# Order of the matmuls within a product, their waits, and the step that makes w_lo

## The chip, the cores and the metric

The kernel runs on one core of a Trainium2 chip. The metric is the device time in microseconds (us). Before the change it is 218.35 us, the median of three runs (217.48 to 218.54).

## What is computed

The reference is one dense layer of a recommendation model for a batch of 512:

```python
sparse_embed = emb_tables[field_idx[None, :], x_sparse]     # 512 x 26 x 64, gathered rows
z = sparse_embed.reshape(B, N_FIELDS * K)                   # 512 x 1664
gram = jnp.einsum('bik,bjk->bij', sparse_embed, sparse_embed)
inner = gram[:, iu, ju]                                     # 512 x 325, pairs i < j
dnn_in = jnp.concatenate([x_dense, z, inner], axis=-1)      # 512 x 2002
h = jax.nn.relu(dnn_in @ w1 + b1)                           # w1 is 2002 x 2002, float32
out = jax.nn.sigmoid(h @ w2 + b2)                           # 512 x 1
```

## The kernel before

The batch is four tiles of 128 (bt 0 to 3). The contraction is 16 row tiles t: 13 of embedding values (z), 3 of inner products, which also hold the dense features and the bias. The 2002 output columns are two halves h (1002 and 1000), and each half is two PSUM banks q of 500 or 502 columns. A piece is one (t, h) part of w1, 128 x 1002 or 128 x 1000 floats. There are 64 pieces, as all of w1 is read twice: phase A serves bt 0 and 1, phases B1 and B2 serve bt 2 and 3. A product is one piece for one bt; there are 128 of them.

Each product is made in float32r with both operands split into a high and a low part. ScalarE casts a piece into w_hi (L843) and the transposed embeddings into x_hi (L869, for inner products L861); VectorE subtracts to get w_lo (L925, two steps per piece, one for each q) and x_lo (L955). TensorE then runs six matmuls for a product (L1062): for each q, w_hi by x_hi, w_lo by x_hi, w_hi by x_lo. Ahead of them it waits for x_lo of its key (x_split, L1044) and, ahead of each q, for that q's w_lo (w_split, L1060):

```python
pe.wait_ge(x_split, x_lo_count(*key_of(step)))
...
for q, cols in enumerate(CHUNK_COLS[h]):
    pe.wait_ge(w_split, 2 * RANK[n] + q + 1)
    for m, (x, w) in enumerate(((xh, hi), (xh, lo), (xl, hi))):
        last = nc.tensor.matmul(slot[s][:, q * BANK:...], x, w[:, cols], ...)
```

The embedding rows come by 104 gathers (indirect DMAs, L819) on GpSimd's queue, four for a group of four fields and one bt (an arrival), each followed by a small memset (L827) that paces the queue. There are 28 arrivals: the sixteen first hold all of bt 0 and 1 and the last field group of bt 2 and 3. Ahead of the seventeenth, GpSimd waits for the fourth gram round (L817). Ahead of arrival k it also waits until arrival k - 5 has been transposed. VectorE transposes an arrival ("turn", L942), ScalarE makes x_hi of it, VectorE x_lo.

The inner products are eight gram rounds on TensorE (L1035). They read ET, copies of the transposed embeddings made by ScalarE (L874) and VectorE (L960), and write PSUM; ScalarE and VectorE copy the results to G (L887, L973), and they come back as rows of x_in by way of DMAs on SP. Before the first round of a pair of tiles, the finished z part of a cell is moved out of its PSUM slot ("park", L879 and L964). A finished cell is drained by VectorE (relu, times w2, sum: L999).

SP loads the pieces into five raw buffers (w_raw); load m waits until both w_lo steps of piece m - 5 are done (L772). There are seven buffers of w_hi and w_lo; ScalarE's cast of piece m waits until the last product of piece m - 7 is done (L842).

The order of every engine's queue is fixed when the program is built, by a planner (`make_orders`, L214). It plays the engines against each other with given durations (`PE_LEN`, `ACT_LEN`, `DVE_LEN`, L196 to L198), takes among the next six steps of TensorE one whose operands are there (`pe_ready`, L378), and on ScalarE and VectorE the operation that is due first (`wanted`, L412, with a lead for each kind). The program then waits on semaphores for what is really done; a queue never changes its order at run time.

## Time and profile before

| | |
|---|---|
| device time, median of 3 | 218.35 us |
| span of the profiled execution | 227.2 us |
| TensorE matmul busy | 206.2 us (91%), 1340 instructions |
| VectorE busy | 147.2 us (65%), 345 instructions |
| ScalarE busy | 129.9 us (57%), 258 instructions |
| GpSimd busy | 129.8 us (57%), 210 instructions |
| DMA | 39.00 MB, mean 172 GB/s |
| mean granted TensorE clock | 0.970 |

The profiled execution's own time is its span, from the first to the last instruction of one execution; it is 8.85 us above the median of the timed runs. In the rows, PE is TensorE's matmuls, PEld its weight loads, DVE is VectorE, ACT is ScalarE, POOL is GpSimd, SP is SyncE. L with a number is a line of the kernel. A matmul of 500 columns shows 0.39 us, but they are pipelined, and the next one starts about 0.228 us after it. "Idle before" is idle time of the engine just ahead of the group's instructions, and the arrow names what ended it.

### The profile page before, as it was taken

The page shows a single profiled execution, that of the slowest core. Times are in us where ns is not written, and L with a number is a line of the kernel's source. Part 1 is how long each engine was busy: PE and PEld are TensorE (multiplying, and loading weights), DVE is VectorE, ACT ScalarE, POOL GpSimd, SP SyncE. Part 2 cuts the span into 40 slices and gives each one's busy share as a digit, 9 for nine tenths or more (in the row PEclk, how much of TensorE's full clock was granted, in tenths as well). Part 3 has the DMA queues.
Part 4 walks back from the last instruction along what each step waited for, and adds up shares of the span by engine and source line. Part 5 has one row for each costly group of instructions (what it writes and reads, how often), then busy time and mean ns, then how long its engine had stood idle before and what let it go on. Part 6 is the DMA issues. An engine that isn't in the chain of part 4 may idle for free.

```text
span 227.2 us, 3900 instructions
## 1 busy us (share of the span) xinstructions
PE 206.2 (91%) x1340; PEld 165.2 (73%) x1340; DVE 147.2 (65%) x345; ACT 129.9 (57%) x258; POOL 129.8 (57%) x210
## 2 busy tenths in 40 slices
PE   8899969989999838999989799599999999999994
PEld 8747848866877626886868588478887887878883
DVE  3596638677638323768829698387587967773274
ACT  2684533788559313979356754389778848462201
POOL 5788878888888880003978888888888500000000
PEclk9999999999999965999999999969999999999999
DMA  5675999883748310224794663668968455304100
GB/s 175 196 242 140 353 356 314 257 288 109 247 143 258 137 26 6 90 48 119 193 340 117 209 198 118 204 192 284 326 208 273 124 176 178 93 15 77 34 0 0
DMA packets 15388, 39.00 MB, mean 172 GB/s; under 512 B 3881, under 2 KB 5281, under 8 KB 15369
## 3 DMA queue, kind: packets, MB, share of 16 engines
q1 hardware_dynamic: 11688, 35.27, 47.4%
q0 software_dynamic: 3328, 3.41, 7.3%
q8 instruction: 10, 0.16, 0.3%
q10 hardware_dynamic: 353, 0.08, 0.2%
q14 instruction: 9, 0.07, 0.1%
HBM read 37.71 MB, written 0.69 MB: 169 GB/s over the span
## 4 chain that ended last, share of the span: by engine, by line
PE 63%; POOL 16%; issue 9%; DMA 7%; DVE 3%; ACT 1%; POOLq 0%; DVEq 0%; ACTq 0%
PE slot L1062 58%; POOL E L819 14%; DMA E<-emb,row_idx 6%; PE slot L1035 5%; POOL pace L827 2%; DVE G L973 1%; DMA x_idx<-idx 1%; DVE slot L999 1%; DVE x_lo L955 0%; ACT w_hi L843 0%; DVE ET L960 0%; DVE T L942 0%; ACT x_hi L869 0%; ACT result L898 0%; DVE wrap L905 0%
## 5 line engine op out<-in xcount | busy, mean ns | idle before, releaser
L819 POOL DMA_INDIRECT E<-emb,row_idx x104 | 112.0, 1077 | 49.2 <-issue 20.4
L1062 PE MATMUL slot<-w_hi,x_hi 128*128 128x500 f32 (+6 forms) x256 | 103.7, 405 | 10.9 <-issue 6.3
L1062 PE MATMUL slot<-w_lo,x_hi 128*128 128x500 f32 (+6 forms) x256 | 101.0, 395 | 0.0
L1062 PE MATMUL slot<-w_hi,x_lo 128*128 128x500 f32 (+6 forms) x256 | 100.6, 393 | 0.0
L925 DVE TENSOR_TENSOR w_lo<-w_raw,w_hi 128x500 fp32r<-128x500 f32 (+6 forms) x128 | 80.1, 670 | 19.2 <-ACT w_hi L843 10.6
L843 ACT CAST w_hi<-w_raw 128x1000 fp32r<-128x1000 f32 (+6 forms) x64 | 65.5, 1029 | 31.9 <-DMA w_raw<-w 14.4
L1062 PEld LDWEIGHTS slot<-w_hi,x_hi 128*128 128x128 f32 (+3 forms) x256 | 49.0, 191 | 26.0 <-issue 9.4
L1062 PEld LDWEIGHTS slot<-w_hi,x_lo 128*128 128x128 f32 (+3 forms) x256 | 49.1, 192 | 10.2
L1062 PEld LDWEIGHTS slot<-w_lo,x_hi 128*128 128x128 f32 (+3 forms) x256 | 49.2, 192 | 9.4 <-issue 0.2
L874 ACT COPY ET<-T 32x128 f32<-32x128 f32 (+4 forms) x90 | 32.5, 362 | 2.1
L942 DVE STREAM_TRANSPOSE T<-E 128x256 f32<-128x256 f32 x24 | 10.6, 442 | 18.4 <-DMA E<-emb,row_idx 13.2
L869 ACT CAST x_hi<-T 128x256 fp32r<-128x256 f32 x24 | 9.7, 406 | 20.1 <-DVE T L942 14.5
L973 DVE COPY G<-slot 26x208 f32<-26x208 f32 x31 | 11.5, 369 | 10.0 <-PE slot L1035 9.0
L1035 PE MATMUL slot<-ET 64*64 64x52 f32 x512 | 11.9, 232 | 6.1 <-issue 5.6
L1035 PEld LDWEIGHTS slot<-ET 64*64 64x64 f32 x512 | 10.0, 145 | 10.0 <-issue 8.7
L827 POOL MEMSET pace<- 128x64 f32 x100 | 16.7, 167 | 0.1
L887 ACT COPY G<-slot 26x208 f32<-26x208 f32 x33 | 10.7, 324 | 10.3 <-PE slot L1035 9.5
L960 DVE COPY ET<-T 32x128 f32<-32x128 f32 (+3 forms) x54 | 13.7, 253 | 1.6
L955 DVE TENSOR_TENSOR x_lo<-T,x_hi 128x256 fp32r<-128x256 f32 x24 | 10.1, 423 | 6.4 <-issue 3.3
L999 DVE SCALAR_TENSOR_TENSOR slot<-slot,w_all 128x500 f32<-128x500 f32 (+1 forms) x16 | 10.8, 688 | 2.3 <-PE slot L1062 2.1
L1007 PE MATMUL slot<-ones 128*128 128x128 f32 x50 | 8.0, 338 | 1.0 <-POOL ones L809 1.0
L1007 PEld LDWEIGHTS slot<-ones 128*128 128x128 f32 x50 | 7.8, 252 | 1.0 <-POOL ones L809 1.0
(33 smaller groups left out, 40.1 us busy)
## 6 DMA issues: line engine op xcount, KB each, us to landing
w_raw<-w SPq DMA_DIRECT2D x32, 501.0 KB
w_raw<-w SPq DMA_DIRECT2D x32, 500.0 KB
E<-emb,row_idx POOLq DMA_INDIRECT x104
w_all<-w SPq DMA_DIRECT2D x1, 1001.0 KB
gram_dram<-G SPq DMA_DIRECT2D x8, 84.5 KB
x_in<-gram_dram SPq DMA_DIRECT2D x8, 42.0 KB
x_in<-G SPq DMA_DIRECT2D x4, 58.5 KB
x_in<-G SPq DMA_DIRECT2D x4, 19.5 KB
```

The costliest lines, as they stand in the source:

```text
L819: nc.gpsimd.indirect_dma_start(out=E[:, k % ER, j, :], out_offset=None, in_=emb_rows, in_offset=bass.IndirectOffsetOnAxis(ap=row_idx[:, at ...
L827: nc.gpsimd.memset(pace[:], 0.0).then_inc(paced, 1)
L843: nc.scalar.copy(w_parts(m)[0], w_source(m)).then_inc(w_hi_ready, 1)
L874: nc.scalar.copy(*et_copy(bt, part, i, h, half)).then_inc(et_by_act, 1)
L887: nc.scalar.copy(gram_place(bt % 2, s, rnd), gram_view(bt, s, b)).then_inc(g_copied_act, 1)
L925: nc.vector.tensor_tensor(lo[:, cols], w_source(m)[:, cols], hi[:, cols].bitcast(F32), ALU.subtract)\
L960: nc.vector.tensor_copy(*et_copy(bt, part, i, h, half)).then_inc(et_by_dve, 1)
L973: nc.vector.tensor_copy(gram_place(bt % 2, s, rnd), gram_view(bt, s, b)).then_inc(g_copied_dve, 1)
L999: nc.vector.scalar_tensor_tensor(out=acc, in0=acc, scalar=0.0, in1=w2_all[:, at:at + width], op0=ALU.max, op1=ALU.mult, accum_out=parts[:, ...
L1007: nc.tensor.matmul(slot[0][:, 0:P], ones[:], ones[:], start=True, stop=True)
L1035: last = nc.tensor.matmul(slot[AUX[bt]][64 * c:64 * c + 64, at:at + 2 * FIELDS], e.rearrange("k s f -> k (s f)"), e[:, :, 0:FIELDS], start ...
L1062: last = nc.tensor.matmul(slot[s][:, q * BANK:q * BANK + CHUNKS[h][q][1]], x, w[:, cols], start=(first and m == 0), stop=(end and m == 2))
```

## The change

In a product that does not end its PSUM cell, the six matmuls are reordered: both q of w_hi by x_hi first, then both q of w_lo by x_hi, then both q of w_hi by x_lo. Each pair has the waits of its own operands only: x_hi and w_hi, then w_lo, then x_lo. A product that ends its cell keeps the old order by q, behind one wait for x_lo and one for w_lo. VectorE makes w_lo of a piece in one step of 1002 or 1000 columns where it made it in two, so 64 steps stand where 128 stood, and w_split counts pieces. The planner gets the new length of that step (1.22 for 0.70 twice), lets a product start once its high parts are there and its low parts come 0.91 (x_lo) and 0.45 (w_lo) later at most, and has smaller leads for hi, lo, turn, x24, x_hi and x_lo. So the fixed orders of the queues can differ too.

```diff
-DVE_LEN = {"lo": 0.70, "turn": 0.46, ...}
+DVE_LEN = {"lo": 1.22, "turn": 0.46, ...}
 HOP = 0.08
+X_LO_LATE, LO_LATE = 0.91, 0.45
@@ pe_ready
             m = rank[s[1]]
-            needs = [("x_lo",) + key_of(s), ("lo", m, 0)]
-            if ("lo", m, 1) not in done:
+            late = {("x_lo",) + key_of(s): X_LO_LATE, ("lo", m): LO_LATE}
+            if any(x not in done for x in late):
                 return None
             c = cell_at(s)
+            needs = [("x_hi",) + key_of(s), ("hi", m)]
+            if s == cells[c][-1]:
+                late = dict.fromkeys(late, 0.0)
...
-            return None if at is None else max(at, done["lo", m, 1] - 0.65) + HOP
+            return None if at is None else max(at, max(done[x] - by for x, by in late.items())) + HOP
@@ wanted
         if kind == "hi":
-            return step_at(uses[pieces[op[1]]], 1.9)
+            return step_at(uses[pieces[op[1]]], 1.35)
         if kind == "lo":
-            return step_at(uses[pieces[op[1]]], 0.75)
+            return step_at(uses[pieces[op[1]]], 0.4)
...
-            tail = {"turn": 2.6 if key[1] == LAST else 1.5, "x24": 1.8, "x_hi": 1.0, "x_lo": 0.5}[kind]
+            tail = {"turn": 2.1 if key[1] == LAST else 1.1, "x24": 1.3, "x_hi": 0.6, "x_lo": -0.3}[kind]
@@ SP
-                        sp.wait_ge(w_split, 2 * (m - RAW + 1))
+                        sp.wait_ge(w_split, m - RAW + 1)
@@ VectorE
-                    m, q = op[1:]
-                    if q == 0:
-                        dve.wait_ge(w_hi_ready, m + 1)
+                    m = op[1]
+                    dve.wait_ge(w_hi_ready, m + 1)
                     hi, lo = w_parts(m)
-                    cols = CHUNK_COLS[PIECES[USED[m]][2]][q]
-                    nc.vector.tensor_tensor(lo[:, cols], w_source(m)[:, cols], hi[:, cols].bitcast(F32), ALU.subtract)\
-                      .then_inc(w_split, 1)
+                    nc.vector.tensor_tensor(lo, w_source(m), hi.bitcast(F32), ALU.subtract).then_inc(w_split, 1)
@@ TensorE
-                    pe.wait_ge(x_split, x_lo_count(*key_of(step)))
...
-                    for q, cols in enumerate(CHUNK_COLS[h]):
-                        pe.wait_ge(w_split, 2 * RANK[n] + q + 1)
-                        for m, (x, w) in enumerate(((xh, hi), (xh, lo), (xl, hi))):
-                            last = nc.tensor.matmul(slot[s][:, q * BANK:q * BANK + CHUNKS[h][q][1]], x, w[:, cols],
-                                                    start=(first and m == 0), stop=(end and m == 2))
-                        if q == 0 and end:
-                            last.then_inc(half_done, 1)
+                    if end:
+                        pe.wait_ge(x_split, x_lo_count(*key_of(step)))
+                        pe.wait_ge(w_split, RANK[n] + 1)
+                        for q in (0, 1):
+                            nc.tensor.matmul(acc[q], xh, hi[:, cols[q]], start=first, stop=False)
+                            nc.tensor.matmul(acc[q], xh, lo[:, cols[q]], start=False, stop=False)
+                            last = nc.tensor.matmul(acc[q], xl, hi[:, cols[q]], start=False, stop=True)
+                            if q == 0:
+                                last.then_inc(half_done, 1)
+                    else:
+                        pe.wait_ge(x_hi_ready, x_hi_count(*key_of(step)))
+                        pe.wait_ge(w_hi_ready, RANK[n] + 1)
+                        for q in (0, 1):
+                            nc.tensor.matmul(acc[q], xh, hi[:, cols[q]], start=first, stop=False)
+                        pe.wait_ge(w_split, RANK[n] + 1)
+                        for q in (0, 1):
+                            nc.tensor.matmul(acc[q], xh, lo[:, cols[q]], start=False, stop=False)
+                        pe.wait_ge(x_split, x_lo_count(*key_of(step)))
+                        for q in (0, 1):
+                            last = nc.tensor.matmul(acc[q], xl, hi[:, cols[q]], start=False, stop=False)
```

## Rows read from the trace of the kernel before

**Rows 1.** The page: shares of the chain that ended last, by engine.
```profile
PE 63%; POOL 16%; issue 9%; DMA 7%; DVE 3%; ACT 1%; POOLq 0%; DVEq 0%; ACTq 0%
```

**Rows 2.** Groups by line: names, count | busy us, mean ns | idle before, releasers.
```profile
L1062 PE MATMUL slot<-w_hi,x_hi 128*128 128x500 f32 (+6 forms) x256 | 103.7, 405 | 10.9 <-issue 6.3 <-DVE x_lo L955 4.5
L925 DVE TENSOR_TENSOR w_lo<-w_raw,w_hi 128x500 fp32r<-128x500 f32 (+6 forms) x128 | 80.1, 670 | 19.2 <-ACT w_hi L843 10.6 <-issue 8.3
L955 DVE TENSOR_TENSOR x_lo<-T,x_hi 128x256 fp32r<-128x256 f32 x24 | 10.1, 423 | 6.4 <-issue 3.3 <-ACT x_hi L869 3.0
```

**Rows 3.** Timeline round a stall of TensorE: start us, us, what, idle before.
```profile
32.48 0.41 ACT L869 CAST x_hi<-T 128x256 fp32r<-128x256 f32 x1 [3.58 <-DVE T L942]
32.92 0.41 DVE L955 TENSOR_TENSOR x_lo<-T,x_hi 128x256 fp32r<-128x256 f32 x1
33.39 0.49 PE L1062 MATMUL slot<-w_hi,x_hi 128*128 128x500 f32 x1 [2.17 <-DVE x_lo L955]
```

**Rows 4.** Timeline of GpSimd and VectorE: a gather beside w_lo, one without.
```profile
34.44 1.85 DVE L925 TENSOR_TENSOR w_lo<-w_raw,w_hi 128x500 fp32r<-128x500 f32 x3
35.78 1.33 POOL L819 DMA_INDIRECT E<-emb,row_idx  x1 [0.27 <-issue]
...
76.05 0.95 POOL L819 DMA_INDIRECT E<-emb,row_idx  x1 [0.27 <-issue]
```

**Rows 5.** Windows for L925 (VectorE): stretch, us, busy (count), clock, DMA share, GB/s.
```profile
5.00:70.00 65.00, 29.66 (x48) 1.00 0.75 243
105.00:172.00 67.00, 32.38 (x52) 0.97 0.69 218
```

**Rows 6.** The same windows for L819, GpSimd's gathers.
```profile
5.00:70.00 65.00, 46.55 (x44) 1.00 0.75 243
105.00:172.00 67.00, 48.45 (x43) 0.97 0.69 218
```

**Rows 7.** Timeline of GpSimd: the longest gather.
```profile
109.35 4.10 POOL L819 DMA_INDIRECT E<-emb,row_idx  x1 [0.27 <-issue]
```

**Rows 8.** Windows: us, busy PE, PEld, DVE, ACT, POOL, clock, DMA; last, ScalarE's timeline.
```profile
78.40:81.80 3.40, 0.11 (x1) 0.02 (x1) 0.85 (x2) 0.57 (x1) 2.58 (x6) 0.83 0.08 19
81.80:87.70 5.90, 3.56 (x65) 2.52 (x65) 0.70 (x2) 0.40 (x1) 3.14 (x6) 0.50 0.21 25
...
80.18 0.57 ACT L879 COPY parked<-slot 128x500 f32<-128x500 f32 x1 [4.19 <-remote]
```

**Rows 9.** Timeline: the last arrival of bt 0, from its last gather to its product.
```profile
67.68 0.95 POOL L819 DMA_INDIRECT E<-emb,row_idx  x1 [0.27 <-issue]
71.84 0.44 DVE L942 STREAM_TRANSPOSE T<-E 128x256 f32<-128x256 f32 x1
73.09 0.41 ACT L869 CAST x_hi<-T 128x256 fp32r<-128x256 f32 x1
74.26 0.39 PE L1062 MATMUL slot<-w_hi,x_hi 128*128 128x500 f32 x1
```

**Rows 10.** Timeline: another arrival, its last gather and its transpose.
```profile
130.08 0.95 POOL L819 DMA_INDIRECT E<-emb,row_idx  x1 [0.27 <-issue]
133.16 0.45 DVE L942 STREAM_TRANSPOSE T<-E 128x256 f32<-128x256 f32 x1 [0.22 <-issue]
```

**Rows 11.** Timeline: arrival 26 of 28, last gather to first product, w_lo ahead.
```profile
166.57 1.02 POOL L819 DMA_INDIRECT E<-emb,row_idx  x1 [0.27 <-issue]
170.10 1.27 DVE L925 TENSOR_TENSOR w_lo<-w_raw,w_hi 128x502 fp32r<-128x502 f32 x2
171.29 0.44 DVE L942 STREAM_TRANSPOSE T<-E 128x256 f32<-128x256 f32 x1
172.22 0.41 ACT L869 CAST x_hi<-T 128x256 fp32r<-128x256 f32 x1
173.18 0.49 PE L1062 MATMUL slot<-w_hi,x_hi 128*128 128x500 f32 x1
```

**Rows 12.** Windows, all engines, columns as in rows 8: behind TensorE's longest stall at an arrival.
```profile
150.00:155.00 5.00, 5.00 (x19) 4.09 (x18) 2.77 (x6) 4.01 (x7) 4.18 (x7) 0.76 0.93 317
```

11 lines of the change are left out of this document (6 added, 5 removed).

## The prediction

> **What bounds the kernel now.** I read the chain of work that ended last, then the groups by line, the timeline at each stall of TensorE, and last the windows and timelines of the gathers. The chain gives TensorE 63%, GpSimd 16% and DMA 7% [rows 1]: TensorE works, and at its stalls it waits for embeddings, whose pace GpSimd sets. The products have 10.9 us of idle time ahead of them [rows 2]. I went through their starts one by one: at eleven of 128 an x_lo ended 0.05 to 0.07 us before the product began, at one a w_lo was as close, and at all others both operands had long been there. A stall in full: x_hi from 32.48 to 32.89, x_lo from 32.92 to 33.33, first matmul at 33.39 [rows 3]. So the end is set by a relay: gathers, transpose, x_hi, x_lo, product. It has two legs. The first ends with the last arrival of bt 0, which the first gram round needs. The fourth round then lets GpSimd start on bt 2 and 3, and the second leg ends at arrival 26, at 173.18 [rows 11]. Behind it TensorE is short of nothing for more than 0.1 us up to the end.
>
> **The profiled execution.** It spans 227.2 us, the median is 218.35. From 78.4 to 81.8 nearly every engine but GpSimd stands still, ScalarE's park waits 4.19 us for a release that no record explains, the granted clock is then 0.50 (1.2 GHz), and the first gram round takes 5.9 us [rows 8], where the later ones take 1.2. That is some 3.4 + 4.7 us, and 1.5 us more in the next two products: about 9.6 us that I take to be of this execution. Without it the span would be 217.6, which fits the median. So I work out a difference and set it against both: span 227.2 and median 218.35.
>
> **Part 1, the high parts first.** At a stall for x_lo, the first matmul can start when x_hi is done, earlier by one x_lo and its hop, 0.44 us at 33.39 and 0.49 at 173.18, if the 0.06 us from release to start stay [rows 3, 11]. The low pair is wanted 4 x 0.228 + 0.10 (a first matmul after a stall takes 0.49, not 0.39 [rows 3, 9]) = 1.01 us later, by when x_lo is there. The gain of one stall does not add to that of the next: the next arrival comes when the gathers bring it, and TensorE waits for it longer by what it won. It adds only where TensorE's own progress sets the next arrival, by way of released w buffers and ScalarE's queue. In the first leg this happens between 50.6 and 74.3: four starts (50.61, 56.91, 68.66, 74.26) hang on casts that wait for released pieces, and the gains add to about 1.4 us if the gathers come as now. In the second leg only the last stall counts: 0.5 us, as x_hi ends at 172.63 and the product starts at 173.18 [rows 11].
> A product has four waits for three. The gap across a wait that is already met is 228 ns (median over 128), like the gaps without one (227 to 229), so I cost it at nothing, at most 5 ns x 128 = 0.6 us. The number of matmuls and weight loads stays. Each pair now goes to two banks in turn; across a change of bank the gap is 227 ns today, so nothing again.
>
> **Part 2, one w_lo step.** Two steps in a row take 1.27 us [rows 11]. The slope from 256 to 500 columns is (670 - 423)/244 = 1.01 ns a column [rows 2], so one step of 1000 takes about 0.67 + 0.51 = 1.18 us. VectorE saves 0.09 us x 64 = 5.8 us of 147, most of it where it is idle: worth at most 0.3 us, beside 107 us, where it works without a pause. w_lo is complete at w_hi + 1.25 and wanted at start + 0.57; the tightest four products (105 to 111 us) lose or win 0.1 us, ahead of a stall that takes it in.
> But the step is now twice as long, and GpSimd feels it. A gather takes 0.95 us when VectorE makes no w_lo. The one at 35.78 takes 1.33: the running w_lo ended at 34.44 + 1.85 = 36.29, and the gather ended 0.82 us after that, at 37.11 [rows 4]. The same 0.82 or 0.83 stands behind most of the gathers over 1.0 us, some three dozen: a gather that needs its operand while a w_lo or x_lo step runs waits for the end of that step. Transposes, copies and drains beside a gather leave it at 0.95.
> The Trainium skill's page "SBUF — State Buffer", section "Who interferes with whom", has the rule: a VectorE instruction with two SBUF inputs contends with a GpSimd instruction that reads SBUF, and whoever has the shared port keeps it for the whole instruction. It speaks against this change, and the trace agrees with it (1.33 against 0.95 us). The same section says that tensor_tensor was seen not to stall DMA issue; by that sentence no gather would grow and the result would be that of rival A, below.
> Price, first leg (5 to 70 us): 44 gathers take 46.55 us, 44 x 0.95 = 41.8, so 4.75 us are holds [rows 6]. By chance alone w_lo, busy 29.66 of 65 us [rows 5], would give 44 x 0.456 x half of 0.67 = 6.7, x_lo 0.6 more; the measured part is 0.65 of that. With 24 steps of 1.18 the same sum is 44 x 0.44 x 0.59 + 0.6 = 12.0, times 0.65 = 7.8: 3.1 us later. Second leg (105 to 172 us): 48.45 - 43 x 0.95 = 7.6 us, of which one gather holds 3.15 [rows 6, 7]; the other 4.45 are 0.58 of 7.7; with 26 steps 12.5 x 0.58 = 7.3: 2.8 us later. Bounds of each: below, no growth at all (holds may stay short if the planner puts the steps elsewhere); above, the factor with the long one counted, 0.99, which gives 4.7.
> Slack on the way. First leg: the last gather of the arrival ends at 68.63, the transpose starts at 71.84 [rows 9]; 2.1 us between the two are enough elsewhere (131.03 to 133.16) [rows 10], so 1.1 us are slack. x_hi starts at 73.09 though the transpose ended at 72.28: 0.8 slack. The product starts at 74.26, 0.76 after x_hi: 0.7 with part 1. Together 2.6. Against it stands that a transpose can now be stuck behind a step of 1.18, not of 0.67, on average 0.25 longer. So 3.1 + 0.2 - 2.6 = 0.7 us late, and the 1.4 us of part 1 are gone: they are in front of a wait that now ends later. The gram rounds and the release of the gathers move by the same 0.7. Second leg: 2.8; slack at the transpose 0.2 (w_lo ran until 171.37; the bound is 1.6), at x_hi 0.45, by part 1 0.5 [rows 11]; a longer w_lo ahead of the transpose adds 0.1. That is 1.75 us late.
>
> **Part 3, the planner.** The order of the queues changes in ways that rows of before can't show. Leads shrink together by 0.35 to 0.8 us, so copies to ET and of the gram come relatively sooner. x_lo's shrinks most: once a step of 1.18 is put ahead of it, it comes 0.6 us later than the matmuls want it, and that stall's gain is gone. I take zero, and 1 us to either side.
>
> **Sum.** 0.7 + 1.75 = 2.45 us: 227.2 to 229.7 for a profile with the same disturbance, and 218.35 to 220.8 for the median.
>
> **Rivals.** A, faster: the gathers are not held longer. Then the first leg gives 1.4 and the second 0.5: 216.4. For it speaks that three gathers (106.6, 108.0, 147.9) ran 0.95 us although a w_lo step covered their start; against it, the thirty-odd that fit. It decides by the holds: the legs break even when they grow by 3.4 us together, not by 5.9, so when a hold by the long step is about 1.35 times one by the short step, not 1.8. B, no change: the holds grow, but the packets are what is late. Landing takes 3.7 us at arrival 26 where 2.1 is possible, while DMA is 0.69 busy on average [rows 5, 11]; if the slack is 1.6 us there and not 0.2, and TensorE's chain rather than the gathers carries the first leg, 2.45 shrinks to between 0 and 1: 218.6. C, slower still: later arrivals make TensorE's stalls longer. The stall at 145 to 148 us was 2.9 us idle, the clock went to 1.2 GHz for part of the next 5 us (0.76 on average) [rows 12], and two products took 1.3 us more. The stall at 31 us (2.2 us) would reach the same length with 1 us more. One or two such stretches in front of waits that do not hide them, or a bad order by the planner: 222.5 to 224. D, the change doesn't do what it says: w_lo becomes the late operand. It needs w_lo late by over 0.57 us behind w_hi at many products, while w_hi is 5 to 20 us ahead at nearly all: no price.
>
> **How the numbers follow.** Forecast 0.48, A 0.27, B 0.14, C 0.11. A difference under 0.5% (1.1 us) can't be told from none in a measurement of this kernel. Faster: A and a little of B, 0.28. Same: most of B and the near edge of the forecast, 0.15. Slower: 0.57. The forecast's own range, from the bounds of the holds (1.5 to 4.7 for each leg) and the planner's 1 us, is 218.9 to 223. With A in it, the range is 216.2 to 223.6.
>
> **What the profile would show.** Right: gathers' mean above 1.15 us for 1.077 now, holds of up to 1.1 us that end 0.82 us after a w_lo step of 1.18 us, arrivals 3 us later at the end of each leg, PE's idle time ahead of the products larger although they start on x_hi. Wrong: a mean of the gathers near 1.08 with TensorE starting 0.06 us after x_hi (rival A); arrivals late by 3 us but product starts unchanged (B); gaps of more than 228 ns inside products would upset part 1.

## The result, and the profile after

| | before | after |
|---|---|---|
| median of the timed runs, us | 217.91 (4 runs, 214.96 to 218.54) | 223.15 (4 runs, 221.36 to 225.64) |
| profiled execution, span, us | 227.2 | 221.2 |
| granted clock of TensorE, mean | 0.970 | 0.982 |

The ratio is 1.0303, 95% interval 1.0244 to 1.0361: the change makes the kernel slower by 3.0%, which is 5.2 us between these medians and 6.6 us by the ratio. The forecast was 220.8, slower by 1.1%. So the side was right, and the size forecast was less than half of the measured one. The ratios here and below leave out executions more than 1.5% slower than the fastest of their kernel; medians and means do not.

The page of after: shares of the chain that ended last (the work followed back from the last instruction), then the groups by line (count | busy us, mean ns of one | idle before, releasers), which answer to [rows 1, 2].

```profile
POOL 49%; PE 29%; issue 11%; DMA 6%; DVE 3%; ACT 1%; POOLq 0%; DVEq 0%
...
L822 POOL DMA_INDIRECT E<-emb,row_idx x104 | 118.8, 1142 | 37.7 <-POOL pace L830 26.5
L1075 PE MATMUL slot<-w_hi,x_hi 128*128 128x500 f32 (+5 forms) x236 | 75.8, 402 | 12.6 <-ACT x_hi L872 10.9
...
L926 DVE TENSOR_TENSOR w_lo<-w_raw,w_hi 128x1000 fp32r<-128x1000 f32 (+6 forms) x64 | 75.3, 1192 | 17.6 <-ACT w_hi L846 17.2
```

GpSimd has 49% of the chain, for 16% in the disturbed profile of before and 36% in an undisturbed one (below). A gather takes 1142 ns in the mean, 1077 before. VectorE's w_lo steps are half as many, 1.19 us each, and cost 75.3 us for 80.1: the 4.8 us saved show, and bring nothing. VectorE's whole busy time fell by only 0.8 us, from 147.2 to 146.4, as the new queues give it more of the copies to ET (16.3 us in 61 for 13.7 in 54). TensorE's products start on x_hi now, as the change says.

The windows of GpSimd's gathers (stretch, us, busy (count), clock, DMA share, GB/s) answer to [rows 6]:

```profile
5.00:70.00 65.00, 47.46 (x42) 0.97 0.72 234
105.00:172.00 67.00, 48.26 (x43) 0.98 0.69 222
```

In the first stretch 42 gathers, of which the last is cut by the edge, take 0.91 us more than 44 took before. What a gather takes longer looks like this, in the timeline of VectorE and GpSimd:

```profile
19.23 1.16 DVE L926 TENSOR_TENSOR w_lo<-w_raw,w_hi 128x1002 fp32r<-128x1002 f32 x1
19.24 1.98 POOL L822 DMA_INDIRECT E<-emb,row_idx  x1 [0.27 <-POOL pace L830]
```

The step ends at 20.39, the gather at 21.22, 0.83 us after it: the same distance as in [rows 4], and the hold is 1.03 us where 0.67 us steps gave 0.4.

The last arrival of bt 0, last gather to product, answers to [rows 9]:

```profile
72.16 1.00 POOL L822 DMA_INDIRECT E<-emb,row_idx  x1 [0.27 <-POOL pace L830]
76.90 0.45 DVE L942 STREAM_TRANSPOSE T<-E 128x256 f32<-128x256 f32 x1 [0.68 <-DMA E<-emb,row_idx]
77.38 0.41 ACT L872 CAST x_hi<-T 128x256 fp32r<-128x256 f32 x1 [0.66 <-DVE T L942]
77.92 0.41 PE L1075 MATMUL slot<-w_hi,x_hi 128*128 128x500 f32 x1
```

Its last gather ends at 73.16, 4.5 us later than the 68.63 of before, and its product starts 3.7 us later. Arrival 26 answers to [rows 11]:

```profile
161.02 1.20 POOL L822 DMA_INDIRECT E<-emb,row_idx  x1 [0.27 <-POOL pace L830]
166.01 0.45 DVE L942 STREAM_TRANSPOSE T<-E 128x256 f32<-128x256 f32 x1 [1.35 <-DMA E<-emb,row_idx]
166.49 0.40 ACT L872 CAST x_hi<-T 128x256 fp32r<-128x256 f32 x1 [1.31 <-DVE T L942]
166.94 0.49 PE L1075 MATMUL slot<-w_hi,x_hi 128*128 128x500 f32 x1 [0.31 <-ACT x_hi L872]
```

Against the first profile of before this can't be compared, as that one holds the disturbance of [rows 8]. A second profile of before (219.43 us, span 217.1, listed with the experiments) has none: its last arrival of bt 0 starts its product at 74.35, the fourth gram round is at 93.69, arrival 26's product at 162.99. After has 77.92, 97.28 and 166.94. So 3.6 us of the 4.1 us between the two spans are made in the first leg, and only 0.4 between the fourth gram round and arrival 26. These are one execution of each kernel. Two stretches of after ran at 1.2 GHz, the first right behind TensorE's longest idle time, the second 1.0 us behind the end of one of 1.68 us. The end of the first idle time in the timeline, and the windows of both stretches (us, busy PE, PEld, DVE, ACT, POOL, clock, DMA share, GB/s):

```profile
35.45 0.90 PE L1075 MATMUL slot<-w_hi,x_hi 128*128 128x500 f32 x2 [3.89 <-ACT x_hi L872]
```

```profile
35.80:39.20 3.40, 3.40 (x10) 2.72 (x9) 3.38 (x4) 2.38 (x3) 3.00 (x4) 0.50 0.94 283
104.10:107.50 3.40, 3.40 (x10) 2.56 (x9) 3.40 (x6) 1.54 (x5) 3.13 (x3) 0.50 0.72 221
```

The second profile of before has one, 138.6 to 142.0, behind an idle time of 2.07 us. Each of these stretches lasts 3.4 us (in some other profiles 6.8, which counts as two) and lowers the mean clock of an execution by 3.4 x 0.5 / 218 = 0.0078. The mean clocks of the timed runs go by about such steps: 0.984, 0.982, 0.977 and 0.969 in after's four, two to four stretches each; in the 79 executions of before that have a clock on record there are 0.5 stretches in the mean, and a clock of 1.000 or close to it is the commonest.

### The profile page after: what moved, and what is told of

It is laid out like the page before. It is cut to its first block, busy times and chain, and to the rows that moved or that the text cites. A ratio compares the mean times of both kernels' runs of the same rounds, so it can differ in the third digit from the quotient of the medians.

```text
span 221.2 us, 3836 instructions
## 1 busy us (share of the span) xinstructions
PE 203.5 (92%) x1340; PEld 163.1 (74%) x1340; DVE 146.4 (66%) x290; ACT 125.5 (57%) x249; POOL 136.6 (62%) x210
## 4 chain that ended last, share of the span: by engine, by line
POOL 49%; PE 29%; issue 11%; DMA 6%; DVE 3%; ACT 1%; POOLq 0%; DVEq 0%
POOL E L822 43%; PE slot L1075 8%; PE slot L1078 7%; PE slot L1081 7%; POOL pace L830 6%; DMA E<-emb,row_idx 5%; PE slot L1035 4%; DVE G L973 2%; PE slot L1067 1%; PE slot L1065 1%; PE slot L1066 1%; DMA x_idx<-idx 1%; DVE slot L999 1%; DVE T L942 0%; ACT x_hi L872 0%
## 5 line engine op out<-in xcount | busy, mean ns | idle before, releaser
L822 POOL DMA_INDIRECT E<-emb,row_idx x104 | 118.8, 1142 | 37.7 <-POOL pace L830 26.5
L1075 PE MATMUL slot<-w_hi,x_hi 128*128 128x500 f32 (+5 forms) x236 | 75.8, 402 | 12.6 <-ACT x_hi L872 10.9
L926 DVE TENSOR_TENSOR w_lo<-w_raw,w_hi 128x1000 fp32r<-128x1000 f32 (+6 forms) x64 | 75.3, 1192 | 17.6 <-ACT w_hi L846 17.2
L1081 PE MATMUL slot<-w_hi,x_lo 128*128 128x500 f32 (+5 forms) x236 | 73.8, 394 | 0.0
L1078 PE MATMUL slot<-w_lo,x_hi 128*128 128x500 f32 (+5 forms) x236 | 73.5, 393 | 0.0
L1075 PEld LDWEIGHTS slot<-w_hi,x_hi 128*128 128x128 f32 (+2 forms) x236 | 43.5, 191 | 25.4 <-ACT x_hi L872 14.7
L1081 PEld LDWEIGHTS slot<-w_hi,x_lo 128*128 128x128 f32 (+2 forms) x236 | 44.5, 191 | 10.2 <-DVE x_lo L955 1.4
L1078 PEld LDWEIGHTS slot<-w_lo,x_hi 128*128 128x128 f32 (+2 forms) x236 | 45.0, 191 | 9.3
L942 DVE STREAM_TRANSPOSE T<-E 128x256 f32<-128x256 f32 x24 | 10.6, 444 | 26.5 <-DMA E<-emb,row_idx 26.3
L960 DVE COPY ET<-T 32x128 f32<-32x128 f32 (+4 forms) x61 | 16.3, 267 | 1.9
L973 DVE COPY G<-slot 26x208 f32<-26x208 f32 x32 | 11.9, 371 | 5.3 <-PE slot L1035 4.4
L890 ACT COPY G<-slot 26x208 f32<-26x208 f32 x32 | 10.4, 324 | 5.2 <-PE slot L1035 4.5
L955 DVE TENSOR_TENSOR x_lo<-x_in,x_hi 117x128 fp32r<-117x128 f32 (+2 forms) x12 | 3.4, 286 | 8.9 <-ACT x_hi L864 8.9
L864 ACT CAST x_hi<-x_in 117x128 fp32r<-117x128 f32 (+2 forms) x12 | 3.4, 297 | 10.1 <-DMA x_in<-gram_dram 5.7
```

The lines of the kernel that those rows point to most:

```text
L822: nc.gpsimd.indirect_dma_start(out=E[:, k % ER, j, :], out_offset=None, in_=emb_rows, in_offset=bass.IndirectOffsetOnAxis(ap=row_idx[:, at ...
L926: nc.vector.tensor_tensor(lo, w_source(m), hi.bitcast(F32), ALU.subtract).then_inc(w_split, 1)
L955: nc.vector.tensor_tensor(lo, src, hi.bitcast(F32), ALU.subtract).then_inc(x_split, 1)
L960: nc.vector.tensor_copy(*et_copy(bt, part, i, h, half)).then_inc(et_by_dve, 1)
L973: nc.vector.tensor_copy(gram_place(bt % 2, s, rnd), gram_view(bt, s, b)).then_inc(g_copied_dve, 1)
L1075: nc.tensor.matmul(acc[q], xh, hi[:, cols[q]], start=first, stop=False)
```

## The experiments

Names with b_ are made from the kernel before, with a_ from the changed one. Each ratio is to the kernel before, in paired runs of the same chip, with its 95% interval; it need not equal the ratio of the medians. "Excess" is the sum over 104 gathers of what each took beyond 0.949 us, from the profiled execution.

| kernel | w_lo step | halves and release | high parts first | leads | ratio | mean, excess of gathers, us | half-clock stretches | against before at full clock, us |
|---|---|---|---|---|---|---|---|---|
| before (second profile) | 500 | apart | no | old | 1 | 1.080, 13.6 | 0.5 | 0 |
| b_high | 500 | apart | yes | old | 0.9916 [0.9880, 0.9952] | 1.051, 10.6 | 0.4 | -2.3 |
| b_ready | 500 | apart | yes, planner told | old | 0.9873 [0.9807, 0.9939] | 1.049, 10.4 | 0.9 | -2.9 |
| b_leads | 500 | apart | yes, planner told | new | 0.9898 [0.9853, 0.9943] | 1.052, 10.7 | 0.9 | -2.1 |
| a_leads_two | 500 | together | yes | old | 1.0019 [0.9984, 1.0054] | 1.062, 11.8 | 0.7 | -0.6 |
| a_two | 500 | together | yes | new | 1.0084 [1.0047, 1.0122] | 1.085, 14.2 | 1.2 | 0.0 |
| a_four | 250 | together | yes | new | 1.0277 [1.0229, 1.0325] | 1.114, 17.1 | 2.2 | +4.7 |
| a_leads | 1000 | one step | yes | old | 1.0237 [1.0160, 1.0314] | 1.162, 22.1 | 2.5 | +3.2 |
| after | 1000 | one step | yes | new | 1.0303 [1.0244, 1.0361] | 1.142, 20.1 | 2.8 | +3.6 |
| b_one | 1000 | one step, before's queues | no | old | 1.0303 [1.0236, 1.0369] | 1.118, 17.5 | 2.7 | +5.1 |
| b_high_one | 1000 | one step, before's queues | yes | old | 1.0360 [1.0293, 1.0427] | 1.109, 16.6 | 1.9 | +5.1 |
| a_onein | 1000, one operand | one step | yes | new | 1.0150 [1.0073, 1.0227] | 1.027, 8.1 | 2.4 | -0.3 |
| b_shift | 500 | apart | no | old | 1.0077 [1.0039, 1.0115] | 1.070, 12.6 | 1.2 | +0.9 |
| b_high_shift | 500 | apart | yes | old | 0.9977 [0.9939, 1.0015] | 1.054, 10.9 | 0.9 | -0.9 |
| a_two_shift | 500 | together | yes | new | 1.0048 [1.0009, 1.0088] | 1.083, 14.0 | 1.5 | +0.1 |

"Half-clock stretches" is the mean over a kernel's executions of (1 - mean clock) / 0.0078. The last column fits all 193 executions at once, one level for each kernel and one common price of a stretch: 1.33 us (standard error 0.12; the levels are good to some 0.5 us). Over the 152 executions that are left without those that the ratios leave out, the price is 0.75 us; the levels of after, a_leads and a_onein then lie 0.8 to 1.2 us higher (4.8, 4.0 and 0.8), that of b_one stays, and that of b_high_one falls to 4.3. The most that 3.4 us at half the clock can cost TensorE is 1.7. The price also holds lateness that came before a stretch, so it bounds what the clock does rather than proves it.

**The length of the step alone.** a_two is the changed kernel with the w_lo step issued as two instructions in a row, one release behind the second. Queues, waits and planner stay.

In the cuts of code from here on, "..." stands for lines left out, and indents are dropped where a cut stands alone.

```diff
-nc.vector.tensor_tensor(lo, w_source(m), hi.bitcast(F32), ALU.subtract).then_inc(w_split, 1)
+width = HALF_W[PIECES[USED[m]][2]]
+cuts = [width * n // 2 // 2 * 2 for n in range(2)] + [width]
+for a, b in zip(cuts, cuts[1:]):
+    last = nc.vector.tensor_tensor(lo[:, a:b], w_source(m)[:, a:b], hi[:, a:b].bitcast(F32), ALU.subtract)
+last.then_inc(w_split, 1)
```

> The changed kernel with its queues, waits and order of matmuls untouched, but each w_lo step issued as two instructions of 500 columns in a row, with one release at the end. Theory (a gather is held until the end of the w_lo instruction it meets): gathers go back to a mean of 1.07 to 1.09 us from 1.142, and the time falls from about 3% over the kernel before to between 1% below and 0.5% above it. Rival (the new orders of the queues, or the waits, cost the time): the time stays 2.5 to 3% over the kernel before, whatever the gathers do.

Measured: 1.0084, the gathers' mean is 1085 ns. VectorE works 4.4 us more than in after and the kernel is 2.2% faster. So of the 3.0% some 2.2 hang on the instruction's length. A second pair says the same: a_leads 1.0237 and a_leads_two 1.0019, again 2.2%. At full clock the two pairs differ by 3.6 and 3.8 us, and the long step brings 1.6 and 1.7 stretches at half clock more. The rival "the holds don't grow, or don't matter" falls.

**One part of the change at a time.** b_one: before's queues and order of matmuls, the whole w_lo made where the first half stood, nothing where the second stood. The waits of SP and TensorE count pieces instead of halves.

```diff
...
                     if q == 0:
                         dve.wait_ge(w_hi_ready, m + 1)
-                    hi, lo = w_parts(m)
-                    cols = CHUNK_COLS[PIECES[USED[m]][2]][q]
-                    nc.vector.tensor_tensor(lo[:, cols], ...).then_inc(w_split, 1)
+                        hi, lo = w_parts(m)
+                        nc.vector.tensor_tensor(lo, w_source(m), hi.bitcast(F32), ALU.subtract).then_inc(w_split, 1)
...
```

> The kernel before with its queue orders and its order of matmuls; only w_lo of a piece is made in one instruction, at the place of the first of the two. Theory of the holds: gathers' mean rises to about 1.14 us, time 1.5 to 3.5% above the kernel before. Rival (orders of the queues): within 0.5% of before.

b_high: before with the changed kernel's TensorE block (high by high on x_hi and w_hi, then w_lo, then x_lo), and two w_lo steps as before. Against the changed kernel's block only the count waited for differs:

```diff
-    pe.wait_ge(w_split, RANK[n] + 1)
+    pe.wait_ge(w_split, 2 * (RANK[n] + 1))
```

> The kernel before with its queue orders and two w_lo steps per piece; only TensorE's order within a product and its waits are those of the change. Expected by my accounting of the stalls: products at a stall start 0.06 us after x_hi instead of after x_lo, time 0.3 to 0.9% below before. Rival (four waits for three, and pairs that go to two banks in turn, cost something): 0 to 1% above before, and gaps inside products above 228 ns.

Measured: b_one 1.0303, b_high 0.9916. The two edits have opposite signs: the order of the matmuls alone gains 0.84%, some 1.8 us, and the one step alone costs what the whole change costs. So neither the new queue orders nor the planner's new start rule is needed for the loss.

**Both, in the queues of before.** b_high_one is b_high with b_one's edit of VectorE.

> Both parts of the change on TensorE and VectorE (high parts first, w_lo of a piece in one instruction at the place of the first of the two), but the queue orders of the kernel before. If the parts add: 0.8% below plus 3.0% above, so 2.0 to 2.5% above before, gathers' mean 1.11 to 1.14 us. If the new queue orders carry a share of the changed kernel's 3.0%, this one is clearly under it; if they carry none, it is at 3.0%.

Measured: 1.0360. Queues made by the planner of before don't save the change. With the short steps the order high first gains 0.84%; with the long step it can't be told from nothing (b_high_one 1.0360 beside b_one 1.0303). That fits a chain set by the gathers: 49% of after's chain is GpSimd, and a start on x_hi only lengthens TensorE's wait for the next arrival.

**Shorter still.** a_four: as a_two, with four instructions of 250 columns; the edit against a_two:

```diff
-cuts = [width * n // 2 // 2 * 2 for n in range(2)] + [width]
+cuts = [width * n // 4 // 2 * 2 for n in range(4)] + [width]
```

> The changed kernel with each w_lo step issued as four instructions of 250 columns, one release at the end. Theory of the holds: a hold is at most about 0.4 us, gathers' mean 1.02 to 1.05 us, time 0 to 1.5% below the same kernel with two instructions, unless VectorE, which gets some 10 us more work, takes it back. Rival: no difference from two instructions, or slower.

Measured: 1.0277, a miss: 1.9% slower than a_two. Two things are new. VectorE's w_lo costs 88.8 us for 79.7. And the longest gathers are longer than any 0.41 us instruction can explain, in the timeline of GpSimd and VectorE:

```profile
100.37 4.91 POOL L822 DMA_INDIRECT E<-emb,row_idx  x1 [0.27 <-POOL pace L830]
...
100.22 1.40 DVE L929 TENSOR_TENSOR w_lo<-w_raw,w_hi 117x250 fp32r<-117x250 f32 x4
101.53 0.28 DVE L959 TENSOR_TENSOR x_lo<-x_in,x_hi 117x128 fp32r<-117x128 f32 x1
101.73 2.72 DVE L929 TENSOR_TENSOR w_lo<-w_raw,w_hi 123x250 fp32r<-123x250 f32 x8
```

The gather passed the ends of twelve instructions and ended at 105.28, 0.83 us after the end of the thirteenth, at 104.45. So a hold is not always until the end of the running instruction; it can last to the end of an unbroken train of instructions, each starting before the one ahead of it has ended. The last section comes back to this. How much of the 1.9% is this, how much the longer VectorE time, and how much the clock (2.2 stretches for 1.2) was not separated.

**Is it the second operand?** a_onein: as after, with w_lo made as w_raw times a constant, one operand in place of two. The low part of the weights is not computed in this kernel.

```diff
-nc.vector.tensor_tensor(lo, w_source(m), hi.bitcast(F32), ALU.subtract).then_inc(w_split, 1)
+nc.vector.tensor_scalar(lo, w_source(m), 0.0001, None, ALU.mult).then_inc(w_split, 1)
```

> The changed kernel with w_lo made by an instruction that reads one operand, w_raw times a constant, instead of w_raw minus w_hi: so the low part of the weights is wrong, and everything else is there, with the same queues, waits and counts. Theory (a step with two operands in SBUF holds the gather): no gather is held by these steps, only by x_lo, mean 0.96 to 0.99 us, time 1.5 to 4% below the kernel before. If the holds are there with one operand too, or grow, the second operand is not the cause, and the gathers keep a mean of about 1.14 us. VectorE's step may also be shorter, which the trace will show.

Measured: 1.0150, the step takes 705 ns for 1192. The gathers are still held, as beside this one:

```profile
32.87 1.36 POOL L822 DMA_INDIRECT E<-emb,row_idx  x1 [0.27 <-POOL pace L830]
...
32.73 1.27 DVE L926 TENSOR_SCALAR w_lo<-w_raw 128x1002 fp32r<-128x1002 f32 x2
```

The first of the two steps ends at 33.41, the gather at 34.23, 0.82 us behind it. So an instruction with one operand in SBUF holds a gather just as well; my expectation that it would not fell. The Trainium skill, page "SBUF — State Buffer", section "Who interferes with whom", allows for that: it says that tensor_scalar too can enter a mode that takes the shared port. The excess, 8.1 us, is the lowest of all, and yet the kernel is 1.5% slower than before (four executions). The clock is the likely reason: 2.4 stretches at half clock in an execution, the one in its profile at 33.8, behind an idle time of 2.27 us that ends at 32.41; at full clock the fit puts it 0.3 us below before (0.8 above, with the lower price of a stretch). So the loss seems to have two sources, the holds and the half clock, and this kernel has mainly the second. It also shows that the stretches can be as many as in the long-step kernels while the holds are the shortest of all: what brings them is not the holds alone.

**The rest: the two halves as one block, and the leads.** b_ready is b_high with the changed planner's start rule and the leads of before; w_lo's halves are still placed one by one.

```diff
...
-            needs = [("x_lo",) + key_of(s), ("lo", m, 0)]
+            late = {("x_lo",) + key_of(s): 0.91, ("lo", m, 1): 0.45}
...
+            needs = [("x_hi",) + key_of(s), ("hi", m)]
```

> High parts first with two w_lo instructions per piece, and a planner that knows the new start of a product (0.91 and 0.45 us for the low parts) but keeps the old leads and lengths. If the planner's new rule for starts helps or is harmless: 0.5 to 1.5% below before, like the kernel with the old orders. If that rule is what makes the orders of the changed kernel worse: 0.5 to 1% above before.

b_leads is b_ready with the leads of the change.

```diff
...
-            return step_at(uses[pieces[op[1]]], 1.9)
+            return step_at(uses[pieces[op[1]]], 1.35)
...
-            return step_at(uses[pieces[op[1]]], 0.75)
+            return step_at(uses[pieces[op[1]]], 0.4)
...
-            tail = {"turn": 2.6 if key[1] == LAST else 1.5, "x24": 1.8, "x_hi": 1.0, "x_lo": 0.5}[kind]
+            tail = {"turn": 2.1 if key[1] == LAST else 1.1, "x24": 1.3, "x_hi": 0.6, "x_lo": -0.3}[kind]
```

> High parts first, two w_lo steps per piece that the planner places one by one, its new rule for starts, and now the smaller leads of the change as well. If the leads do the harm that is left beside the long instruction (0.8% over before instead of 1.3% below it): 0.5 to 1% above before. If the harm is that the w_lo of a piece is one uninterrupted block in VectorE's queue: 1 to 1.5% below before.

a_leads is the changed kernel with that last diff taken back.

> The changed kernel with the planner's leads (hi, lo, turn, x24, x_hi, x_lo) put back to those of the kernel before; one w_lo instruction, high parts first, new rule of when a product may start. If the smaller leads cost the time beside the holds: 0.5 to 1.5% below the changed kernel, so 1.5 to 2.5% over before. If not: 3.0% again.

a_leads_two is a_leads with a_two's edit.

> The mirror of it: the old leads, but w_lo of a piece as one block of the queue, in two instructions in a row with one release. If the block does the harm: 0.5 to 1% above before. If the leads do: about 1% below before.

Measured: b_ready 0.9873, b_leads 0.9898, a_leads 1.0237, a_leads_two 1.0019. Three pairs for the leads (b_ready and b_leads, a_leads_two and a_two, a_leads and after) put the new ones 0.25, 0.65 and 0.65% slower; in the second the intervals just touch, in the others they overlap widely. And from b_ready to a_leads_two, where the instructions have the same length, 1.5% are lost; from b_leads to a_two 1.9%. What differs is that the two are one block with one release, and with it the order of all queues that the planner makes for a block.

I first read this as the price of the block: the transpose of arrival (0, 3) goes between the halves in b_ready, and in a_two it waits behind two whole pieces, each behind its own w_hi. VectorE in b_ready, then in a_two:

```profile
53.66 0.68 DVE L928 TENSOR_TENSOR w_lo<-w_raw,w_hi 128x500 fp32r<-128x500 f32 x1 [0.18 <-ACT w_hi L846]
54.26 0.44 DVE L945 STREAM_TRANSPOSE T<-E 128x256 f32<-128x256 f32 x1
54.62 0.64 DVE L928 TENSOR_TENSOR w_lo<-w_raw,w_hi 128x500 fp32r<-128x500 f32 x1
```

```profile
57.57 1.27 DVE L929 TENSOR_TENSOR w_lo<-w_raw,w_hi 128x500 fp32r<-128x500 f32 x2 [0.87 <-ACT w_hi L846]
58.75 0.44 DVE L946 STREAM_TRANSPOSE T<-E 128x256 f32<-128x256 f32 x1
```

**The same kernel in a second profile.** a_two_again is a_two, unedited.

> The changed kernel with w_lo in two instructions, unedited, for a second profile. Its first profile lost 3.2 us against that of the kernel with the same leads and the halves apart (transpose of arrival (0, 5) at 74.65 against 71.44; fourth gram round at 95.70 against 91.81), while the holds up to there differed by 1.5 us only, and later one gather of 4.69 us came at 101.94. Theory 'the block': the transpose of (0, 5) is at 74.0 to 75.2 again and that of (0, 3) at 58 to 59 behind two whole pieces, the fourth round at 95 to 96; the long gather may or may not be there, the end moves by less than 3 us with it. Rival 'one long hold and chance': the fourth round is at 92 to 93, and what the time loses comes with a gather of over 2.5 us. Time 216.5 to 219.5 us by the first, below 216 by the second when no long gather shows. Third reading: if the long gather is again near 102 us, it belongs to this kernel as the one of before does to it.

Measured: 216.20 us, beside 216.62 of before on the same chip, one execution of each. The fourth gram round starts at 92.76, not 95.70, and the transpose of (0, 3) at 55.31. So the rival was right for the first leg: what the first profile of a_two had lost there is not the block's. The long gather is there again, 3.50 us at 100.51, as by the third reading. Where the two profiles part shows at the product of arrival (1, 2). TensorE in a_two and the window behind it, then the same in a_two_again:

```profile
51.87 0.49 PE L1079 MATMUL slot<-w_hi,x_hi 128*128 128x500 f32 x1 [2.07 <-ACT x_hi L872]
...
51.80:55.20 3.40, 3.33 (x9) 2.75 (x10) 2.38 (x7) 2.29 (x6) 2.59 (x7) 0.59 0.24 77
```

```profile
49.86 0.50 PE L1079 MATMUL slot<-w_hi,x_hi 128*128 128x500 f32 x1
...
51.80:55.20 3.40, 3.40 (x16) 2.83 (x15) 2.81 (x6) 3.12 (x4) 2.86 (x5) 1.00 0.24 40
```

The last gather of that arrival ended 0.89 us later (46.19, 45.30), its rows landed 2.0 us later (50.39, 48.37), TensorE idled 2.07 us, and then ran at 0.59 of its clock: 9 matmuls in 3.4 us where the other execution has 16. The casts that wait for freed w pieces came late, and with them w_lo and the transpose of (0, 3), by 3.4 us. At the fourth round 2.9 of the 3.4 us were left. So one kernel, in two executions, went from 0.9 us at a last gather to 3 us at the fourth round; the order of events suggests that the stall and the half clock made the difference, and no run separates them. A half-clock stretch doesn't follow every idle time of this length: a_two_again has 2.53 us at 33.13 with no drop of the clock behind it.

Both profiles of a_two hold one gather for long, 4.69 us at 101.94 and 3.50 at 100.51, as do the one of a_leads_two (3.50 at 99.51) and both of before; b_high, b_ready and b_leads have none over 1.6 us there. But the gather that before's profiles hold for long, the fourth behind the fourth gram round, is caught in them too. In b_high:

```profile
97.29 1.26 DVE L925 TENSOR_TENSOR w_lo<-w_raw,w_hi 117x500 fp32r<-117x500 f32 x2
97.84 1.53 POOL L819 DMA_INDIRECT E<-emb,row_idx  x1 [0.27 <-POOL pace L827]
99.31 0.29 DVE L955 TENSOR_TENSOR x_lo<-x_in,x_hi 117x128 fp32r<-117x128 f32 x1 [0.76 <-ACT x_hi L861]
```

It starts 0.04 us ahead of the second w_lo, as the one at 99.86 in before's second profile does, and ends 0.82 us after that w_lo. Here x_lo comes 0.76 us later (0.3 in b_leads, 0.1 in b_ready) and VectorE pauses; in before x_lo and four more w_lo follow without a pause, and the gather is held through all of them. So in these profiles the catch is the same and the pause on VectorE goes with its end. a_leads_two and b_ready, both at full clock throughout, are level at the fourth round (91.81, 91.71), 1.85 us apart after the long gather (last gather of (3, 0): 107.18, 105.33), and 2.3 us in their spans. The block's 1.5 to 1.9% could be this one hold, and so could the 0.84% for the high parts first.

**The long hold, moved.** Three kernels put one more memset on GpSimd ahead of each of the gathers 57 to 60: b_shift from before, a_two_shift from a_two, b_high_shift from b_high.

```diff
+SHIFTED = (57, 58, 59, 60)
...
                     if at > SOON:
+                        if at in SHIFTED:
+                            nc.gpsimd.memset(shift[:, at - SHIFTED[0], :], 0.0)
                         nc.gpsimd.memset(pace[:], 0.0).then_inc(paced, 1)
```

> The kernel before with one more memset of 128x64 (some 0.17 us) on GpSimd ahead of each of the gathers 57 to 60, nothing else. These are the gathers at 97 to 101 us, where gathers and VectorE's w_lo, w_lo, x_lo run at the same period (1.39 us) and, in two profiles of two, gather 59 starts 0.04 us ahead of a w_lo step and is held for 4.09 us. The memsets cost at most 0.8 us and move the starts against VectorE's steps by 0.2 to 0.8 us. Theory 'the long hold is a coincidence of starts and carries 2 to 3 us to the end': no gather over 2 us near 100 us, and the kernel is FASTER than before though work was added, ratio 0.988 to 0.994. Rival 'the long hold is hidden or made up later': ratio 1.000 to 1.004. Third: another gather is caught in place of this one, a long hold stays, ratio 1.000 to 1.004.

> The changed kernel with w_lo in two instructions (block, one release) and the same four memsets. In its two profiles a gather at 101.94 and 100.51 was held for 4.69 and 3.50 us. Theory 'the 1.9% between this kernel and the one with the halves apart is mostly this one hold': with the hold gone it falls from 1.0084 to 0.994 to 1.000. Rival 'the block costs by late transposes and x_lo': it stays at 1.005 to 1.012 though the hold is gone.

> Control: the kernel before with high parts first, whose profile has no long hold, with the same four memsets. They can only cost: 0 to 0.8 us on top of 0.9916, so 0.991 to 0.996. If it gets slower by more than 1 us, the shift by itself has a price or brings a long hold into this kernel. If b_shift comes out as fast as this one, high parts first was worth nothing by itself and its 0.84% was the missing hold; if b_shift stays 0.5% or more behind, the order has a worth of its own.

Measured: 1.0077, 1.0048 and 0.9977. The edit was too blunt. Each memset costs only 0.09 us (two of them start 0.09 apart), but b_shift still has a gather of 2.24 us at 99.20 between two of 1.45, and a_two_shift one of 4.01 at 102.12. So nothing follows on what the long hold is worth; by its gathers the third reading of b_shift's expectation fits, though 1.0077 lies above the 1.004 that it allowed. The control got slower by 0.6%, 1.3 us, for 0.36 us of work, over the bound of 1 us that I had set for "the shift has a price of its own" (the intervals of b_high and b_high_shift just touch), without a long hold and at full clock in its profile. What does follow: with the same shifts in both, b_high_shift stays 1.0% ahead of b_shift, so that high parts first, with short steps, is ahead of before in two pairs out of two. As b_shift still has its gather of 2.24 us and b_high_shift has none over 1.45, this does not tell the order's own worth from that of the hold either. And a_two_shift is as fast as a_two within the intervals.

**Before, once more.** before_again is the kernel before, unedited.

> The kernel before, unchanged, profiled again. The first profile held a stand-still at 78 us, a stretch at half clock behind it and one gather of 4.10 us. If all three are of that one execution, the span is 213 to 216 us, every gather ends within 0.5 us of its 0.95, and the fourth gram round starts at 92 to 94 us. If the long gather belongs to the kernel, it stands again at the same place and the span is 217 to 218.

Measured: 219.43 us, at the upper end of its runs. The long gather of [rows 7] is there again at the same place of the program; the standstill and the half clock of [rows 8] are not, so those were of one execution, as the prediction took them (it put 9.6 us on them, and the two spans differ by 10.1), while the long gather belongs to the kernel in two profiles of two. After's profile doesn't have it: its longest hold in that leg is 1.24 us.

Of all versions b_ready has the lowest ratio, 1.3% under before and 4.2% under after, though its interval overlaps those of b_leads and b_high: high parts first, two w_lo steps, each at a place of its own.

## Why the prediction was right or wrong

**What bounds the kernel: right.** The relay of gathers, transpose and x_hi sets the time, and the change moved the chain further to GpSimd (49% for 36%). But which arrival sets the first leg can change, see Slack.

**Part 1: right in its steps.** At after's nine stalls of over 0.3 us the product starts 0.05 us after x_hi. The stride inside a product stays 227 to 229 ns, so the four waits cost nothing and the order of banks nothing. The whole is -0.84% with short steps (b_high), 1.8 us where the prediction had 1.4 + 0.5 = 1.9 before it struck out the 1.4; how much of the 0.84% is the missing long hold is open. With the long step it is worth nothing that can be told (b_one 1.0303, b_high_one 1.0360), so striking it out was right.

**Part 2, VectorE's gain: right** (1192 ns for the 1.18 us forecast, 4.8 us saved on w_lo for 5.8), and worth nothing.

**Part 2, the holds: the mechanism right, the growth undersized.** Taking the end of a w_lo or x_lo instruction in progress 60 ns after a gather's start, plus 0.82 us, gives the end of 100 of the 104 gathers of after within 25 ns. But the growth in the first leg was 4.6 us, not 3.1: the excess up to the last gather of (0, 5) went from 5.17 to 9.73 us, and its end from 68.63 to 73.16. The step that failed is the factor 0.65 on the chance sum, taken from one execution of before; in after it is about 0.8 (9.7 us for the chance sum of 12.0 of the forecast). For arrivals 16 to 25 the excess is 7.40 and 7.86 us, which looks like no growth. Without before's single hold of 3.15 us it is 4.25 and 7.86: the ordinary holds grew by 3.6 us where 2.8 was forecast. The forecast kept the long hold in both kernels; it vanished in after's profile. Had all executions of before that hold, the second leg would have given the 0.4 us read above. What the faster executions of before have there no profile shows.

**Slack: the term that failed in the first leg.** I took 2.6 us off 3.1 + 0.2. Of 4.5 us at the last gather, 3.7 arrived at the product, so 0.9 in place of 2.6 was taken up on the way. Instead of a transpose at 2.1 us behind its last gather, it came 3.7 us behind, and it did not stand behind w_lo but waited for the rows to land. The distance from gather to transpose, which was to shrink by 1.1 us, grew by 0.5. The two other pieces were found: x_hi starts 0.03 us after the transpose (0.8 us), and from x_hi's start to the product's it is 0.54 us where it was 1.17 (0.6 us). And this arrival did not set the product's start alone. TensorE had worked without a gap since 66.91:

```profile
66.91 0.72 PE L1075 MATMUL slot<-w_hi,x_hi 128*128 128x500 f32 x2 [1.50 <-ACT x_hi L872]
```

Eight products of 1.38 us lead from there to 77.92, so the start is as late as the stall at 66.91 made it. That stall waited for arrival (1, 3), whose last gather ended at 61.05, 4.6 us later than in before, and whose rows landed 3.9 us behind it. The prediction followed the delay along the last arrival alone and had no term for an earlier one. The 2.1 us of [rows 10] was a good case and not a bound: over after's arrivals the distance between the last gather's end and the last of its packets runs from 1.2 to 4.5 us. Rival B named that and used it for the other sign.

**A transpose or x_lo behind w_lo: open.** It was priced at 0.2 and 0.1 us. Over the 24 arrivals of four gathers the time from the end of x_hi to the start of x_lo sums to 11.5 us in before and 11.9 in b_ready, but to 18.3 in a_leads_two and 16.5 in after. It is 16.5 in b_leads too, where the halves are apart, so the smaller leads do it as well as the block. But no run shows that this reaches the end: b_ready and a_leads_two are level at the fourth round. From there on they differ by one long hold.

**Planner: near zero for the leads.** They cost 0.25 to 0.65% by the three pairs, 0.5 to 1.4 us, at the edge of what the pairs tell and of the 1 us allowed. What the planner's orders for a block of w_lo cost beside the long hold was not separated.

**The clock: what the sum lacked.** At full clock the fit puts after 3.6 us (standard error 0.6) above before, or 4.8 with the lower price of a stretch, where the sum had 2.45. The rest of the 6.7 between the means of all executions (223.33, 216.61), 3.1 or 1.9 us, goes with 2.3 more stretches at half clock. This is rival C: it said that longer holds lengthen TensorE's stalls, named the one at 31 us as the next to bring the clock down, and gave 222.5 to 224; measured were 223.15, and the stall at 35.45 was followed by 1.2 GHz. The profiles of all four kernels with a two-operand step of 1000 columns (after, a_leads, b_one, b_high_one) have idle times of 2.97 to 4.69 us that end at 33.9 to 36.3 us, and a mean clock of 0.77 to 0.89 between 30 and 45 us; before has 2.17 us there at most, and full clock. The step that failed is that the sum put the clock at nothing: C was taken as a rival to the holds, with 0.11, though the cause it named was the forecast's own. With 3.1 us of holds forecast ahead of a stall of 2.2 us that "would reach the same length with 1 us more", the forecast should have contained it. That the holds bring the stretches is shown only as far as the pairs go (a_two 1.2, after 2.8, same queues); a_onein has 2.4 with the fewest holds.

**The sum, term by term.** The first leg was put at 0.7 us and came out at 3.6: the growth of the holds was 4.5 for 3.1, and the slack 0.9 for 2.6. The second leg was put at 1.75 and came out at 0.4, against a profile of before with a hold of 4.09 us in it. The two errors partly cancel, which is luck. The clock, 1.9 to 3.1 us over all executions, had no term.

**The other rivals.** A (holds don't grow) falls by a_two. B (packets late anyway) falls in its sign, though its reading of the packets was right. D never shows: at no stall is w_lo the late operand. The marks set for the profile: the mean of the gathers was to pass 1.15 us and just missed it with 1.142; holds of up to 1.1 us came (1.03 at 19.24, 1.24 at 105.69); arrivals 3 us late were 3.6 and 4.

**What stays open.** Whether the one long hold near 100 us makes the difference between the kernels with halves apart and as a block, and how much of the price of a half-clock stretch is the clock's own: only the order of events in one pair of profiles speaks for that. And what brings the stretches in a_onein, where the holds are small.

## What to carry to other kernels

Merging two instructions saves their fixed cost only if their engine is late; here 4.8 us of w_lo time were saved and 3% of the kernel's time lost, some 2.2 of it by the step's length, as a GpSimd gather that starts beside the step is held to its end. By chance the holds sum to the gathers' number times the step's busy share times half its length, so at equal work they grow with the length: 14.2 us with 0.67 us steps and 20.1 with 1.19 (a_two, after). When an edit makes TensorE's waits longer, price the clock behind them as part of the forecast and not as a rival: mean clock and time of every timed run say how often it falls. Slack that one good case shows (2.1 us from gather to transpose) is no slack until the landing times of many are read. And a delay must be followed along every arrival that TensorE waits for, not the last alone.

## What the runs showed of the hardware that was not expected

A few gathers are held far beyond one instruction. In the second profile of before, GpSimd's timeline and VectorE's:

```profile
99.86 4.09 POOL L819 DMA_INDIRECT E<-emb,row_idx  x1 [0.27 <-POOL pace L827]
...
99.31 1.26 DVE L925 TENSOR_TENSOR w_lo<-w_raw,w_hi 117x500 fp32r<-117x500 f32 x2
100.49 0.28 DVE L955 TENSOR_TENSOR x_lo<-x_in,x_hi 117x128 fp32r<-117x128 f32 x1
100.69 2.43 DVE L925 TENSOR_TENSOR w_lo<-w_raw,w_hi 123x500 fp32r<-123x500 f32 x4
```

The gather ends at 103.95, 0.83 us after the end of the last step at 103.12, and passes six ends of instructions on the way, at each of which an ordinary gather would have gone on. Fifteen such gathers stand in the profiles, 1.87 to 4.91 us long, and four more passed one end and took 1.22 to 1.53 us. Twelve of them started within 41 ns of the start of a w_lo or x_lo instruction in an unbroken train: 99.86 beside 99.90 here, 105.69 beside 105.66 in after (2.19 us), 101.94 beside 101.97 in a_two (4.69), four of the five in a_four. Eleven of the fifteen are held until VectorE's train of such steps is over; the four of 2.19 and 2.24 us were let go while it went on. A start that close is not enough for a hold: 99.86's neighbours at 97.08 and 98.47 started as close to one and took 0.95 us. Near 100 us a gather comes every 1.39 us and VectorE repeats w_lo, w_lo, x_lo every 1.38 us (99.31, 100.69), so the starts keep their distance for some turns. Why the moment decides is not known, and the shifts above didn't tell. The section of the Trainium skill's "SBUF — State Buffer" named above says, of a VectorE instruction in a 2-port mode, that whoever issues first gets the shared pair for the whole instruction; most holds here, by steps with two operands, go the same way (0.82 us behind its end), and no sentence of it covers these fifteen.
